# Logarithms of edge counts stored as they are computed, and copied into rows from DRAM to DRAM

## The chip, the cores and the metric

The kernel runs on one core of one Trainium2 chip. The metric is the device time of one execution in microseconds (us). A core has TensorE (PE; its weight loads are shown as PEld), VectorE (DVE), ScalarE (ACT), GpSimd (POOL) and SyncE (SP), and it is served by 16 DMA engines. SPq is SP's own queue of instructions, on which most of this kernel's transfers are issued. On-chip memories are SBUF and PSUM; DRAM is the large memory outside.

## The reference, cut to what matters

A graph of 3125 nodes and 100,000 edges passes through two blocks. Each block holds graph attention, a mixing layer and a feed-forward layer. Four graph attention layers run in all (one in block 0, three in block 1), and all of them use the same edges:

```python
loop = jnp.arange(N, dtype=edge_index.dtype)
src = jnp.concatenate([edge_index[0], loop])
dst = jnp.concatenate([edge_index[1], loop])
alpha = jax.nn.leaky_relu(a_src[src] + a_dst[dst], NEG_SLOPE)
m = jax.ops.segment_max(alpha, dst, num_segments=N)
alpha = jnp.exp(alpha - jax.lax.stop_gradient(m)[dst])
denom = jax.ops.segment_sum(alpha, dst, num_segments=N)
alpha = alpha / (denom[dst] + 1e-16)
out = jax.ops.segment_sum(h[src] * alpha[:, :, None], dst, num_segments=N)
...
x = x + _L0_gnn_ref(xn, ...) + _L0_mix_ref(xn[None], ...)[0]
x = x + _L0_ffn_ref(...)[0]
x = x + _L1_gnn_ref(...) + _L1_mix_ref(...)[0]
x = x + _L1_ffn_ref(...)[0]
```

## The kernel before, in words

The kernel turns the edge list into a dense matrix of 3125 x 3125 edge counts and works with it as a mask: for each pair of target d and source s it needs the negated logarithm of the count, and a very large number where there is no edge. That matrix ("lowered", 39 MB of fp32) is computed once and stored in DRAM. Each attention layer then reads it back in tiles of 125 targets (125 rows of 12,500 bytes, issued at L65 and L66, 50 pairs for each layer with two passes over the heads, 25 for the last layer).

The program is a row of stages. A stage ends when all engines have reached a barrier; SP reaches it after its own last wait. The stages that matter here, in order:

- "codes" and "keys" read the edges and make comparison codes.
- "counts" makes the matrix, one tile t of 125 targets at a time, 25 tiles. VectorE makes one-hot matrices (L303), TensorE multiplies them into counts in PSUM (L317, L320), ScalarE takes logarithm and mask of them (L336, L337) and VectorE subtracts the two (L296). The result is the SBUF tile nl[:, t % 2]: two buffers, each 125 partitions x 25 windows x 125. SP stores it. ScalarE may write tile t only when the store of tile t - 2 has landed in full.
- "general" does the same work for unusual edge lists; a flag tells that it is to be skipped, and with these inputs it is.
- "st0", "nm0", "g0p" and further stages of block 0 normalize, project and run the mixing layer. The first transfer that SP issues in them is the load of the projection's weights (g0p_w).
- "g0a" is the first attention layer (its `g.out` is "relu"). Its SP block begins with the loads of the first two tiles of "lowered".

How a tile is laid out decides the shape of its store. In SBUF, partition p = 25 e + s holds, for every window w and b, the element of target row 5 w + e (e from 0 to 4) and source column 125 s + b. In DRAM "lowered" is stored by rows of 3125. A partition's 3125 numbers thus belong to 25 different rows, and its store is 25 runs of 125 numbers, 500 bytes each. One tile is 3125 such runs, the whole matrix 78,125.

`tile_dma` (L63) splits each store into two transfers, of partitions 0 to 111 (L65) and of the last 13 (L66). `s.sem` makes a semaphore that the stage clears at its end. A transfer adds 16 to its semaphore when it has landed.

Within a stage each engine runs its instructions in the order of the code. SP's order is the order in which transfers enter its queue.

Of the kernel before, what the change touches and what calls it, by code (L numbers as in the profile page):

```python
# [13 lines left out]
N = 3125  # L14
R = 125
T = N // R
# [46 lines left out]
def tile_dma(eng, dst, src, sem):  # L63

    eng.dma_start(dst[0:CUT], src[0:CUT]).then_inc(sem, 16)  # L65
    eng.dma_start(dst[CUT:R], src[CUT:R]).then_inc(sem, 16)  # L66


def wait_apart(eng, tick, sem, value):

    eng.wait_ge(sem, value)
    eng.sem_inc(tick, 1)
# [20 lines left out]
W5 = 5  # L93
# [182 lines left out]
TINY = 2.0 ** -60  # L276


def stage_counts(nc, m, K, own, ownw, steps):

    with Stage(nc, "counts") as s:
        ohb, ohq = s.sb("ohb", [P, 2, 2, PAIRS, R, 2], BF16), s.sb("ohq", [P, 2, 2, PAIRS, QW, 2], BF16)
        nl, ln = s.sb("nl", [R, 2, T, R]), s.sb("ln", [R, 2, T, R])
        ps = s.ps("ps", 7)
        neg = s.sb("neg", [R, 2])
        hot, full, free, both_ready, nl_ready = s.sem("hot"), s.sem("full"), s.sem("free"), s.sem("both_ready"), s.sem("nl_ready")
        nl_out = [s.sem(f"nl_out{n}") for n in range(2)]
        block = s.block()

        @block.vector  # L290
        def _(dve):
            numbers = steps.unsqueeze(1).to_broadcast([P, PAIRS, R, 2])

            def lowered(t):
                dve.wait_ge(both_ready, t + 1)
                nc.vector.tensor_tensor(nl[:, t % 2], nl[:, t % 2], ln[:, t % 2], ALU.subtract).then_inc(nl_ready, 1)  # L296
            for t in range(T):
                if t > 1:
                    dve.wait_ge(full, (t - 1) * 7)
                for c in range(2):  # L300
                    for oh, c0 in ((ohq, 0), (ohb, 2)):
                        code = K[:, c0 + c, t, :].rearrange("p (x y) -> p x y", y=2).unsqueeze(2).to_broadcast([P, PAIRS, R, 2])
                        last = nc.vector.tensor_tensor(oh[:, t % 2, c], code, numbers, ALU.is_equal)  # L303
                last.then_inc(hot, 1)
                if t > 0:
                    lowered(t - 1)
            lowered(T - 1)

        @block.tensor
        def _(pe):  # L310
            for t in range(T):
                pe.wait_ge(hot, t + 1)
                for j, windows in JOBS:
                    w0, nw = windows[0], len(windows)
                    if t > 0:
                        pe.wait_ge(free, (t - 1) * 7 + j + 1)
                    nc.tensor.matmul(ps[0:R, j, 0:nw * R], own[:, t, :], ownw[:, w0:w0 + nw, :].rearrange("p w b -> p (w b)"), start=True, stop=False)  # L317
                    for x, w in enumerate(windows):
                        for c in range(2):
                            last = nc.tensor.matmul(ps[0:R, j, x * R:(x + 1) * R], ohq[:, t % 2, c, w // 2, :, w % 2], ohb[:, t % 2, c, w // 2, :, w % 2],  # L320
                                                    start=False, stop=(x == nw - 1 and c == 1))
                    last.then_inc(full, 1)

        @block.scalar
        def _(act):
            nc.scalar.activation(neg[:, 0:1], m.ones[0:R, 0:1], ACT.Copy, scale=NEG)
            nc.scalar.activation(neg[:, 1:2], m.ones[0:R, 0:1], ACT.Copy, scale=TINY)
            nc.scalar.drain()
            for t in range(T):
                if t > 1:  # L330
                    act.wait_ge(nl_out[t % 2], (t // 2) * 32)
                for j, windows in JOBS:
                    act.wait_ge(full, t * 7 + j + 1)
                    w0, nw = windows[0], len(windows)
                    counted = ps[0:R, j, 0:nw * R].rearrange("p (w b) -> p w b", b=R)
                    nc.scalar.activation(ln[:, t % 2, w0:w0 + nw, :], counted, ACT.Ln, bias=neg[:, 1:2])  # L336
                    nc.scalar.activation(nl[:, t % 2, w0:w0 + nw, :], counted, ACT.Relu, bias=neg[:, 0:1], scale=-NEG).then_inc(free, 1)  # L337
                nc.scalar.drain().then_inc(both_ready, 1)

        @block.sync  # L340
        def _(sp):
            for t in range(T):
                sp.wait_ge(nl_ready, t + 1)
                tile_dma(sp, m.NLQ[:, t], nl[:, t % 2], nl_out[t % 2])
            for n, x in enumerate(nl_out):
                sp.wait_ge(x, 32 * len(range(n, T, 2)))


def stage_counts_general(nc, m, wstart_rows):

    BLOCKS = (EDGES + CAP - 1) // CAP
    with Stage(nc, "general") as s:
        wstart = s.sb("wstart", [P, NW])
        e = s.sb("e", [P, 2, 2])
# [4 lines left out]
        tcol, own = s.sb("tcol", [R, T]), s.sb("own", [R, T])  # L359
        ps = s.ps("ps", 7)  # L360
        loaded, hot, full, added, zeroed = [s.sem(x) for x in ("loaded", "hot", "full", "added", "zeroed")]
        starts_in, counted, logged, finished, out = [s.sem(x) for x in ("starts_in", "counted", "logged", "finished", "out")]
        block = s.block()
        iota = m.iota[:, 0:R]
# [66 lines left out]
        def sp_part(sp):  # L431
            sp.dma_start(wstart[:], wstart_rows).then_inc(starts_in, 16)
            sp.sem_inc(out, 32)
            sp.sem_inc(added, 1)
            with sp.Fori(0, T) as t:
                with sp.Fori(0, BLOCKS) as r:
                    wait_apart(sp, s.tick, added, t * BLOCKS + r + 1)
                    wait_apart(sp, s.tick, zeroed, t + 1)
                    at = sp.snap(r * CAP)
                    sp.dma_start(e[:], m.QB[ds(at, CAP)].rearrange("(p c) k -> p c k", p=P)).then_inc(loaded, 16)  # L440
                wait_apart(sp, s.tick, finished, t + 1)
                tile_dma(sp, m.NLQ[:, ds(t, 1)].rearrange("p o w b -> p (o w) b"), nl[:], out)
            sp.wait_ge(out, 32 + 32 * T)

        @block.sync
        def _(sp):
            either(sp, sp_part)
# [384 lines left out]
def stage_gat_attend(nc, m, g, AL, HX, OUT, X=None, spare=None):  # L832
# [9 lines left out]
    with Stage(nc, g.name + "a") as s:  # L842
        als, nl = s.sb("als", [R, H, N]), s.sb("nl", [R, 2, N])
        as2 = s.sb("as2", [R, HG, N])[:] if spare is None else spare.rearrange("p (h n) -> p h n", h=HG)
        x = s.sb("x", [R, 3, N])
# [5 lines left out]
            low = s.sb("low", [R, 2, W])  # L851
        pst, pso = s.ps("pst", 6), s.ps("pso", 2)
        spread, als_ready = s.sem("spread"), s.sem("als_ready")
        nl_in = [s.sem(f"nl_in{p}") for p in range(2)]
        offset_ready, scaled, masked, exped, turned = [s.sem(n) for n in ("offset_ready", "scaled", "masked", "exped", "turned")]
        weighted, gathered, copied, inverted, rows_free = [s.sem(n) for n in ("weighted", "gathered", "copied", "inverted", "rows_free")]
# [60 lines left out]
        @block.sync  # L917
        def _(sp):
            def counts(gt, p):
                t = gt - gt // T * T if isinstance(gt, int) else gt  # L920
                tile_dma(sp, nl[:, p, :], m.NL[ds(t * R, R)], nl_in[p])
            counts(0, 0)
            counts(1, 1)
            for q in range(PASSES):
                with sp.Fori(0, T // 2 - 1) as i:
                    for p in range(2):
                        wait_apart(sp, s.tick, masked, (q * T + i * 2 + p + 1) * HG)
                        counts(i * 2 + p + 2, (q + p) % 2)
                for t in range(T - 3, T):
                    if q * T + t + 2 < PASSES * T and (t == T - 3 or q < PASSES - 1):  # L930
                        sp.wait_ge(masked, (q * T + t + 1) * HG)
                        counts(q * T + t + 2, (q + t) % 2)
# [222 lines left out]
def graph_attention(nc, m, g, AL, HX, OUT, X=None, spare=None):  # L1155

    stage_gat_attend(nc, m, g, AL, HX, OUT, X, spare)
# [1298 lines left out]
def build(nc, a, out):  # L2456
    m = Machine()
    m.src, m.dst = a["src"], a["dst"]

    def dram(name, shape, dt=F32):  # L2460
        return nc.dram_tensor(name, shape, dt).ap()
    m.QB = dram("edge_codes", [EDGES + CAP, 2])
    m.LO = dram("window_starts", [25, 25], I32)
    m.NL = dram("lowered", [N, N])
    m.NLQ = m.NL.rearrange("d s -> (d s)").rearrange("(t w p b) -> p t w b", t=T, w=T, p=R)
    m.XR, m.YR = dram("normal_rows", [N, D]), dram("expert_rows", [RESULTS, D])
    m.Y, m.XS = dram("attended", [N, 512]), dram("kept_rows", [R, T, D])
    with ExitStack() as ctx:
# [18 lines left out]
        with ExitStack() as cx:  # L2487
# [13 lines left out]
            with ExitStack() as c:  # L2501
                K, steps = sb("K", [P, 4, T, TE], BF16, c)[:], sb("steps", [P, R, 2], BF16, c)[:]
                own, ownw = sb("own", [P, T, R], BF16, c)[:], sb("ownw", [P, T, R], BF16, c)[:]
                stage_keys(nc, m, K, own, ownw, steps, X, x_rows, x_in)
                stage_counts(nc, m, K, own, ownw, steps)
            stage_counts_general(nc, m, a["c_wstart"])

            g0 = Gat("g0", 4, 64, "relu")
# [111 lines left out]
```

## Time and profile before

| | |
|---|---|
| time, median of 3 runs | 5261.91 us (5257.02 to 5267.69) |
| the profiled execution's own time | 5264.06 us |
| its span | 5262.4 us |
| PE / PEld busy | 4553.4 us (87%) / 4129.2 us (78%) |
| DVE busy | 3190.1 us (61%) |
| ACT busy | 2856.9 us (54%) |
| POOL busy | 1455.1 us (28%) |
| DMA queue of SP and ACT (q1) | 181,542 packets, 429.21 MB, 32.6% of 16 engines' time |
| packets under 512 bytes | 108,730 of 197,457 |

The profile was taken from one execution, and its times are inside that execution. A share of an engine's busy time is an average over the whole span. The stages differ, and the stage "counts" takes only about 6% of the span, from about 175 us (the first store) to about 467 us (the last store has landed). The DMA share of a stretch is the time in which the 16 DMA engines had a packet in work, divided by 16 times the stretch. Where packets of one engine overlap, it goes over 1.

### The profile page before, as it was taken

The page shows a single profiled execution, that of the slowest core. Times are in us where ns is not written, and L with a number is a line of the kernel's source. Part 1 is how long each engine was busy: PE and PEld are TensorE (multiplying, and loading weights), DVE is VectorE, ACT ScalarE, POOL GpSimd, SP SyncE. Part 2 cuts the span into 40 slices and gives each one's busy share as a digit, 9 for nine tenths or more (in the row PEclk, how much of TensorE's full clock was granted, in tenths as well). Part 3 has the DMA queues.
Part 4 walks back from the last instruction along what each step waited for, and adds up shares of the span by engine and source line. Part 5 has one row for each costly group of instructions (what it writes and reads, how often), then busy time and mean ns, then how long its engine had stood idle before and what let it go on. Part 6 is the DMA issues. An engine that isn't in the chain of part 4 may idle for free. (4 is left out here: it accounts for less than half of the span.)

```text
span 5262.4 us, 91302 instructions
## 1 busy us (share of the span) xinstructions
PE 4553.4 (87%) x34042; PEld 4129.2 (78%) x34042; DVE 3190.1 (61%) x2697; ACT 2856.9 (54%) x3889; POOL 1455.1 (28%) x1169
## 2 busy tenths in 40 slices
PE   1454669999999859987799999979999999799989
PEld 1443447999999858874489999977999999688755
DVE  4795230688888641116378888853888888255333
ACT  0563322577777523332157787752777877344332
POOL 3001000022222112220126666640566666100000
PEclk9776769899999879997899999989999999899989
DMA  2684000333333155542134434432444344354100
GB/s 49 95 134 77 5 18 0 84 96 96 96 96 96 37 175 173 174 140 50 43 86 104 104 96 104 104 78 64 109 104 104 94 104 104 101 139 115 33 17 20
DMA packets 197457, 462.87 MB, mean 88 GB/s; under 512 B 108730, under 2 KB 145579, under 8 KB 175126
## 3 DMA queue, kind: packets, MB, share of 16 engines
q1 hardware_dynamic: 181542, 429.21, 32.6%
q0 software_dynamic: 15296, 28.83, 2.3%
q8 instruction: 258, 4.23, 0.4%
q14 instruction: 73, 0.60, 0.0%
q10 hardware_dynamic: 288, 0.00, 0.0%
HBM read 388.28 MB, written 69.61 MB: 87 GB/s over the span
## 5 line engine op out<-in xcount | busy, mean ns | idle before, releaser
L1123 PE MATMUL g2a_pso<-HX,g2a_wt 125*125 125x129 f32 x5000 | 603.3, 274 | 7.2 <-DVEq L970 3.9
L1123 PE MATMUL g1a_pso<-HX,g1a_wt 125*125 125x129 f32 x5000 | 603.2, 275 | 4.6 <-ACT g1a_wt L1007 3.3
L1123 PE MATMUL g0a_pso<-HX,g0a_wt 125*125 125x65 f32 x5000 | 595.9, 274 | 5.9 <-ACT g0a_wt L1007 3.3
L1123 PEld LDWEIGHTS g0a_pso<-HX,g0a_wt 125*125 125x125 f32 x5000 | 586.0, 194 | 6.4 <-ACT g0a_wt L1007 3.4
L1123 PEld LDWEIGHTS g2a_pso<-HX,g2a_wt 125*125 125x125 f32 x5000 | 576.7, 189 | 7.6 <-DVEq L970 4.2
L1123 PEld LDWEIGHTS g1a_pso<-HX,g1a_wt 125*125 125x125 f32 x5000 | 576.9, 189 | 5.1 <-ACT g1a_wt L1007 3.5
L1007 ACT ACTIVATE g0a_wt<-g0a_pst 125x1000 f32<-125x1000 f32 (+1 forms) x300 | 312.0, 1040 | 199.8 <-PE g0a_pst L1110 199.8
L940 DVE SCALAR_TENSOR_TENSOR g0a_x<-g0a_als,g0a_cd,HX 125x3125 f32<-125x3125 f32 x100 | 347.5, 3475 | 111.2 <-PE g0a_pst L1110 102.0
L940 DVE SCALAR_TENSOR_TENSOR g2a_x<-g2a_als,g2a_cd,g2a_as 125x3125 f32<-125x3125 f32 x100 | 357.5, 3575 | 83.2 <-PE g2a_pst L1110 73.3
L940 DVE SCALAR_TENSOR_TENSOR g1a_x<-g1a_als,g1a_cd,g1a_as 125x3125 f32<-125x3125 f32 x100 | 358.2, 3582 | 80.6 <-PE g1a_pst L1110 70.4
L1007 ACT ACTIVATE g2a_wt<-g2a_pst 125x1000 f32<-125x1000 f32 (+1 forms) x300 | 312.2, 1041 | 169.6 <-PE g2a_pst L1110 169.6
L1007 ACT ACTIVATE g1a_wt<-g1a_pst 125x1000 f32<-125x1000 f32 (+1 forms) x300 | 312.2, 1041 | 169.5 <-PE g1a_pst L1110 169.5
L945 DVE CUSTOM_DVE_ANT_0 g1a_x<-g1a_x,g1a_nl 125x3125 f32<-125x3125 f32 x100 | 344.9, 3448 | 19.6 <-issue 13.9
L945 DVE CUSTOM_DVE_ANT_0 g2a_x<-g2a_x,g2a_nl 125x3125 f32<-125x3125 f32 x100 | 344.1, 3441 | 19.6 <-issue 13.9
L945 DVE CUSTOM_DVE_ANT_0 g0a_x<-g0a_x,g0a_nl 125x3125 f32<-125x3125 f32 x100 | 341.5, 3415 | 19.6 <-issue 13.9
L1110 PE MATMUL g0a_pst<-C,g0a_x 125*125 125x125 f32 x2500 | 346.0, 284 | 3.6 <-ACT g0a_x L999 3.6
L999 ACT ACTIVATE g2a_x<-g2a_x,g2a_top 125x1000 f32<-125x1000 f32 (+1 forms) x300 | 346.5, 1156 | 3.7 <-DVEq L947 3.7
L999 ACT ACTIVATE g0a_x<-g0a_x,g0a_top 125x1000 f32<-125x1000 f32 (+1 forms) x300 | 346.6, 1156 | 2.4 <-DVEq L947 2.4
L999 ACT ACTIVATE g1a_x<-g1a_x,g1a_top 125x1000 f32<-125x1000 f32 (+1 forms) x300 | 346.6, 1156 | 1.7 <-DVEq L947 1.7
L1110 PE MATMUL g1a_pst<-C,g1a_x 125*125 125x125 f32 x2500 | 323.0, 273 | 3.6 <-ACT g1a_x L999 3.6
L1110 PE MATMUL g2a_pst<-C,g2a_x 125*125 125x125 f32 x2500 | 322.5, 273 | 2.2 <-ACT g2a_x L999 2.2
L1110 PEld LDWEIGHTS g0a_pst<-C,g0a_x 125*125 125x125 f32 x2500 | 305.5, 194 | 3.8 <-ACT g0a_x L999 3.8
(454 smaller groups left out, 8201.5 us busy)
## 6 DMA issues: line engine op xcount, KB each, us to landing
g0a_nl<-lowered SPq DMA_DIRECT2D x50, 1367.2 KB
g1a_nl<-lowered SPq DMA_DIRECT2D x50, 1367.2 KB
g2a_nl<-lowered SPq DMA_DIRECT2D x50, 1367.2 KB
moe_wa<-in_L_ffn_W SPq DMA_DIRECT2D x56, 1024.0 KB, 5.2
lowered<-counts_nl SPq DMA_DIRECT2D x25, 1367.2 KB
g3a_nl<-lowered SPq DMA_DIRECT2D x25, 1367.2 KB
g0a_nl<-lowered SPq DMA_DIRECT2D x50, 158.7 KB
g1a_nl<-lowered SPq DMA_DIRECT2D x50, 158.7 KB
```

The source lines that it names most:

```text
L940: nc.vector.scalar_tensor_tensor(out=x[:, b, :], in0=als[:, h, :], scalar=cd[:, h:h + 1, ds(t, 1)].rearrange("p a b -> p (a b)"), in1=as2[ ...
L945: nc.vector.tensor_tensor_reduce(out=x[:, b, :], in0=x[:, b, :], in1=nl[:, (q + k // HG) % 2, :], scale=1.0, scalar=3e38, op0=ALU.add, op1 ...
L999: nc.scalar.activation(x[:, b, c0:c1], x[:, b, c0:c1], ACT.Exp, bias=top[:, b:b + 1], scale=-1.0).then_inc(exped, 1)
L1007: nc.scalar.activation(wt[:, side, 0:n * R].rearrange("p (b n) -> p b n", b=banks), pst[0:R, 3 * side:3 * side + banks, 0:per * R], ACT.Co ...
L1110: last = nc.tensor.transpose(pst[0:R, 3 * side + j // per, col:col + R], x[:, ring(q, k), (a0 + j) * R:(a0 + j + 1) * R], m.ident[0:R, 0:R])
L1123: last = nc.tensor.matmul(pso[0:R, unit(q, 0, k) % 2, 0:F + 1], wt[:, side, j * R:(j + 1) * R], HX[:, a, q * HG + k % HG, :], start=(a == ...
```

## The change

Four edits are made.

1. A second DRAM tensor, "computed", takes each tile as SBUF holds it: 125 partitions of 12,500 bytes each, one run for a partition. `m.NLQ` is now a view of it.
2. For each tile, five DRAM to DRAM copies (`copy_rows`, one for each e) move it from "computed" into the rows of "lowered". One copy is 25 windows x 25 parts s x 125 numbers: read as 625 runs of 500 bytes that lie 12,500 bytes apart, and written as 25 rows of 12,500 bytes. SP issues the copies of tile t - 1 behind the store of tile t, and first waits until the store of tile t - 1 has landed.
3. The copies count on a semaphore of their own (`by_row`), which outlives the stage. The stage's end no longer waits until the last data is in "lowered". The first attention layer waits for all 125 copies (16 x 5 x 25) before its first load.
4. The skipped stage "general" gets the same copies inside its branch.

```diff
+def copy_rows(sp, m, t, sem):
+    for e in range(W5):
+        sp.dma_start(m.NLR[t, e], m.NLD[t, e]).then_inc(sem, 16)
...
             for t in range(T):
                 sp.wait_ge(nl_ready, t + 1)
                 tile_dma(sp, m.NLQ[:, t], nl[:, t % 2], nl_out[t % 2])
-            for n, x in enumerate(nl_out):
-                sp.wait_ge(x, 32 * len(range(n, T, 2)))
+                if t > 0:
+                    sp.wait_ge(nl_out[(t - 1) % 2], ((t - 1) // 2 + 1) * 32)
+                    copy_rows(sp, m, t - 1, m.by_row)
+            sp.wait_ge(nl_out[(T - 1) % 2], ((T - 1) // 2 + 1) * 32)
+            copy_rows(sp, m, T - 1, m.by_row)
...
+        rows_again = s.sem("rows_again")
...
             sp.wait_ge(out, 32 + 32 * T)
+            sp.wait_ge(m.by_row, 16 * W5 * T)
+            for t in range(T):
+                copy_rows(sp, m, t, rows_again)
+            sp.wait_ge(rows_again, 16 * W5 * T)
...
+        first_layer = g.out == "relu"
+        if first_layer:
+            s.sems.append(m.by_row)
...
+            if first_layer:
+                sp.wait_ge(m.by_row, 16 * W5 * T)
             counts(0, 0)
             counts(1, 1)
...
     m.NL = dram("lowered", [N, N])
-    m.NLQ = m.NL.rearrange("d s -> (d s)").rearrange("(t w p b) -> p t w b", t=T, w=T, p=R)
+    computed = dram("computed", [N * N])
+    m.NLQ = computed.rearrange("(t p w b) -> p t w b", t=T, w=T, p=R)
+    m.NLD = computed.rearrange("(t e s w b) -> t e w s b", t=T, e=W5, s=T, w=T)
+    m.NLR = m.NL.rearrange("(t w e) (s b) -> t e w s b", t=T, e=W5, s=T)
+    m.by_row = nc.alloc_semaphore("by_row")
```

These are SP's instructions at the start of the stage "counts" before the change (a wait in brackets belongs to the instruction beside it; semaphores bear the name of their first user, so codes_counted stands for `nl_ready`, codes_summed and codes_prefix for the two of `nl_out`):

```order
L340 UNCONDITIONAL_BRANCH [waits barrier_Pool_Activation_PE_DVE_SP_release]
L65 DMA lowered<-counts_nl 112x25x125 [waits codes_counted]
L66 DMA lowered<-counts_nl 13x25x125
L65 DMA lowered<-counts_nl 112x25x125 [waits codes_counted]
L66 DMA lowered<-counts_nl 13x25x125
L65 DMA lowered<-counts_nl 112x25x125 [waits codes_counted]
```

And these are SP's instructions at the same place after it:

```order
L65 DMA computed<-counts_nl 112x3125 [waits codes_counted]
L66 DMA computed<-counts_nl 13x3125
L65 DMA computed<-counts_nl 112x3125 [waits codes_counted]
L66 DMA computed<-counts_nl 13x3125
L281 DMA lowered<-computed 25x25x125 [waits codes_summed]
L281 DMA lowered<-computed 25x25x125 x4
L65 DMA computed<-counts_nl 112x3125 [waits codes_counted]
L66 DMA computed<-counts_nl 13x3125
L281 DMA lowered<-computed 25x25x125 [waits codes_prefix]
L281 DMA lowered<-computed 25x25x125 x4
```

The stores lose their middle dimension of 25, and five copies of 25 x 25 x 125 stand between one tile's store and the next.

At the end of the stage, SP had this before:

```order
L65 DMA lowered<-counts_nl 112x25x125 [waits codes_counted]
L66 DMA lowered<-counts_nl 13x25x125
L57 UNCONDITIONAL_BRANCH [waits codes_prefix,codes_summed]
L445 UNCONDITIONAL_BRANCH [waits barrier_Pool_Activation_PE_DVE_SP_release]
L367 TENSOR_LOAD flag
```

and has this now:

```order
L65 DMA computed<-counts_nl 112x3125 [waits codes_counted]
L66 DMA computed<-counts_nl 13x3125
L281 DMA lowered<-computed 25x25x125 [waits codes_prefix]
L281 DMA lowered<-computed 25x25x125 x4
L281 DMA lowered<-computed 25x25x125 [waits codes_summed]
L281 DMA lowered<-computed 25x25x125 x4
L57 UNCONDITIONAL_BRANCH
L458 UNCONDITIONAL_BRANCH [waits barrier_Pool_Activation_PE_DVE_SP_release]
```

The ten copies of the last two tiles stand behind the last store, and the leave from the stage (L57) has no wait of its own any more.

## Rows read from the trace of the kernel before

**Rows 1.** Timeline of SP: start us, duration us; first two and last stores.

```profile
174.65 0.33 SPq L65 DMA_DIRECT2D lowered<-counts_nl  x1
175.02 4.36 SPq L66 DMA_DIRECT2D lowered<-counts_nl  x1
185.01 0.32 SPq L65 DMA_DIRECT2D lowered<-counts_nl  x1
...
455.53 0.32 SPq L65 DMA_DIRECT2D lowered<-counts_nl  x1
455.89 4.68 SPq L66 DMA_DIRECT2D lowered<-counts_nl  x1
```

**Rows 2.** Groups by line, 100 to 700 us: busy us, mean ns, idle before.

```profile
L303 DVE TENSOR_TENSOR counts_ohq<-K,steps 128x3250 bf16<-128x3250 bf16 x50 | 92.2, 1845 | 1.5 <-PEq L60 1.5
L303 DVE TENSOR_TENSOR counts_ohb<-K,steps 128x3250 bf16<-128x3250 bf16 x50 | 92.2, 1845 | 0.0
L296 DVE TENSOR_TENSOR counts_nl<-counts_nl,counts_ln 125x3125 f32<-125x3125 f32 x25 | 85.3, 3413 | 40.0 <-ACTq L338 39.9
```

**Rows 3.** Stretches: us, five engines busy (PE to POOL), clock, DMA share, GB/s.

```profile
175.00:300.00 125.00, 67.07 (x583) 56.59 (x584) 112.86 (x55) 78.01 (x148) 0.00 (x0) 0.73 0.88 136
300.00:462.00 162.00, 83.00 (x731) 70.25 (x729) 130.02 (x62) 96.63 (x182) 0.00 (x0) 0.72 0.86 134
```

**Rows 4.** Waits in 174 to 470 us: total, times, longest.

```profile
ACT counts_ln L336 <- DMA lowered<-counts_nl: 91.1, 21, 8.7
DVE counts_nl L296 <- ACTq L338: 39.9, 16, 9.8
```

**Rows 5.** Waits of SP's queue, 430 to 480 us.

```profile
SPq L57 <- DMA lowered<-counts_nl: 6.8, 1, 6.8
```

**Rows 6.** Timeline behind the stage "counts".

```profile
470.66 8.27 DVE L477 BATCH_NORM_STATS2 st_st<-X 125x6 f32<-125x256 f32 x25 [15.16 <-PEq L60]
493.73 0.83 SPq L722 DMA_DIRECT2D g0p_w<-in_L_gnn_W  x2
935.95 0.34 SPq L65 DMA_DIRECT2D g0a_nl<-lowered  x1
```

**Rows 7.** Stretches of the last store, the first g0a_nl loads, lina_rows loads (1 KB).

```profile
456.50:457.50 1.00, 0.00 (x0) 0.00 (x0) 0.00 (x0) 0.00 (x0) 0.00 (x0) 0.50 1.00 270
459.00:461.00 2.00, 0.00 (x0) 0.00 (x0) 0.00 (x0) 0.00 (x0) 0.00 (x0) 0.50 1.20 150
461.00:463.00 2.00, 0.00 (x0) 0.00 (x0) 0.00 (x0) 0.00 (x0) 0.00 (x0) 0.50 1.20 152
938.00:940.00 2.00, 1.67 (x15) 1.49 (x15) 0.00 (x0) 1.70 (x2) 0.00 (x0) 1.00 1.06 331
2435.50:2436.50 1.00, 0.00 (x0) 0.00 (x0) 0.90 (x2) 0.00 (x0) 0.00 (x0) 0.50 0.26 91
```

**Rows 8.** Stretches with transfers of 125 partitions alone (src/dst loads; edge codes store).

```profile
8.00:9.00 1.00, 0.00 (x0) 0.00 (x0) 0.00 (x0) 0.00 (x0) 0.00 (x0) 1.00 0.32 131
10.00:11.00 1.00, 0.00 (x0) 0.00 (x0) 0.00 (x0) 0.00 (x0) 0.00 (x0) 1.00 0.32 131
...
22.00:24.00 2.00, 0.00 (x0) 0.00 (x0) 1.55 (x3) 0.00 (x0) 0.00 (x0) 1.00 0.31 125
```

**Rows 9.** Timeline of SP: the loads of src and dst.

```profile
4.91 0.34 SPq L123 DMA_DIRECT2D codes_srci<-in_src  x1
5.30 0.30 SPq L124 DMA_DIRECT2D codes_dsti<-in_dst  x1
```

**Rows 10.** Stretches of the first store.

```profile
174.00:176.00 2.00, 0.00 (x0) 0.00 (x0) 2.00 (x2) 2.00 (x5) 0.00 (x0) 1.00 0.21 58
176.00:178.00 2.00, 0.00 (x0) 0.00 (x0) 2.00 (x2) 2.00 (x5) 0.00 (x0) 0.74 1.04 239
178.00:180.00 2.00, 0.00 (x0) 0.00 (x0) 2.00 (x3) 0.68 (x3) 0.00 (x0) 0.50 1.23 154
```

**Rows 11.** The page's DMA queues: packets, MB, share of 16 engines.

```profile
q1 hardware_dynamic: 181542, 429.21, 32.6%
```

## The prediction

> **What bounds the kernel now.** I read the page first. Over the whole span PE leads, but its share says nothing of the stage that is changed, so I went on to the waits, the groups, the stretches and SP's timeline of "counts" alone. The stores begin at 174.65 us and the last is issued at 455.53 us [rows 1]: 280.9 us for 24 tiles, 11.7 us for one. Two limits lie close together there. VectorE has 4 one-hot operations of 1.845 us and one subtraction of 3.413 us in each tile, 10.8 us [rows 2]. The DMA engines are at a share of 0.88 and 0.86, moving 136 and 134 GB/s [rows 3]. ScalarE waited 91.1 us for stores to land, and through it VectorE 39.9 us [rows 4]. So the stores of 500-byte runs do set the pace, but VectorE would take over as soon as they got faster: all that can be won inside the stage is 24 x (11.7 - 10.8) = 22 us. At the end SP waits 6.8 us for the last store [rows 5], and VectorE starts the next stage at 470.66 us [rows 6], 3.3 us after SP is free (455.89 + 4.68 + 6.8 = 467.4).
>
> **What a run costs.** The last store runs alone. Its steady part moves 150 and 152 GB/s over 16 engines [rows 7], so one engine needs 500 x 16 / 151,000 us = 53 ns for a run of 500 bytes. Its first microsecond shows 270 GB/s, or 30 ns.
>
> **The change part by part.**
>
> *The stores* become 125 runs of 12,500 bytes. With 112 partitions over 16 engines and 13 over 13, a busy engine gets 8 partitions, 100 KB. No row shows a store of that shape. The load of the same tile in g0a moves 331 GB/s, 20.7 GB/s for each engine [rows 7], which makes 4.8 us. The store of 125 partitions of edge codes moves 125 GB/s on few engines [rows 8], 25 GB/s each, which makes 4.0 us. I take W = 4.3 us, where the present stores take about 10 us. Taken alone this edit would give back at most the 22 us of the stage and some 5 us at its end.
>
> *The copies* are the heart of it. They bring back all 78,125 runs of 500 bytes, now from DRAM to DRAM, so the question is on how many engines they run. The transfers of 125 partitions in "codes" are the nearest rows: while the loads of src and dst, or the store of the edge codes, are alone, the share stands at 0.32 and 0.31 at 131 and 125 GB/s [rows 8]. That is 5 of 16 engines (0.3125), each fully busy. Stores of 112 partitions use all 16 (share 1.0 and above, rows 7). Five is the largest number up to 16 that divides 125, and 16 is the largest for 112. A copy has 25 windows as its outer dimension on both sides, and for 25 that number is 5 again. And it is the same five each time: src and dst were issued 0.4 us apart [rows 9], and two transfers on different engines would have shown twice the share. So I expect all 125 copies on the same five.
>
> The Trainium skill speaks against this change just there. "DMA: Bandwidth & Descriptors", section "Why a DMA increments its semaphore by 16 and not by 1", says that the number of engines is the largest up to 16 that divides the slowest dimension of both sides, and that the lowest-numbered ones are taken. By that rule, the trace's 0.31 and 0.32 agree with it for 125; that it also holds for copies from DRAM to DRAM with 25, no row of before shows.
>
> For one tile each of these five engines gets 5 x 625 / 5 = 625 runs. The cost of a run from DRAM to DRAM is in no row. Below it is bounded by the 30 ns of the fresh store; above by a read and a write in turn, 53 ns for the write and 47 ns for the read, for which the nearest row is the loads of 1 KB rows to 125 partitions (91 GB/s at share 0.26, so 91 x 0.3125 / 0.26 = 109 GB/s while busy, 22 GB/s for each engine, 47 ns for 1 KB; I take it whole). That makes 100 ns. I take 53 ns, the row with the same size and the same count. Reading and writing can overlap, and five engines press the memory less than sixteen, but each side is scattered, so I do not go below it. C = 625 x 0.053 = 33.1 us for a tile (18.8 us at 30 ns, 62.5 us at 100 ns).
>
> *What the copies hold up.* SP issues the store of tile t behind the copies of tile t - 2, in one queue, and on the five engines it runs behind them. ScalarE needs this store's buffer two tiles later (that is the wait of 91.1 us in rows 4, which now waits behind C). By then VectorE and ScalarE have long finished their 10.8 us. So the copies are not hidden beside the computation: the five engines work without a gap, and a tile takes C + W = 37.4 us in place of 11.7. The other eleven engines stand mostly idle.
>
> *The end of the stage.* SP no longer waits for the last copies, but it must have issued them. Beside the first store the row of L66 lasts 4.36 us [rows 1]: SP was let go at 179.4 us, when about 58 x 2 + 239 x 2 + 154 x 1.4 = 810 KB had moved [rows 10], which is 101 of the 175 runs of each engine. So SP is let go with some 75 runs of the transfer ahead outstanding. Before its last copy that leaves 75 + 125 = 200 runs for each engine, 10.6 us.
>
> *The added waits.* The wait for the store of tile t - 1 ahead of its copies is met by then, since that store lies in the queue ahead of the copies of tile t - 2. Behind it stand only the copies and the next store. The wait of the first attention layer stood at 935.95 us [rows 6] and moves back with everything; the copies have ended by then. Behind it stand the first two tile loads. It costs nothing. The load of g0p_w, 23 us after VectorE's start [rows 6], comes after the last copies too (10.6 us). The untaken branch costs nothing.
>
> **The sum.** The first copies are issued behind the second store (185.01 us, rows 1), which is through by about 190 us. From there: 25 x 33.1 = 828 us of copies and 23 stores x 4.3 = 99 us end at 1117 us; SP is free 10.6 us earlier, and VectorE begins the next stage 3.3 us after that, at 1110 us, against 470.66 us. The change costs 639 us. The profiled execution of before took 5264.06 us, which makes 5903 us; the median of the runs lies 2 us lower, so I predict 5901 us. At 30 ns: 190 + 469 + 99 - 6 + 3 = 755, 285 us more than now, 5547 us. At 100 ns: 190 + 1563 + 99 - 20 + 3 = 1835, 1364 us more than now, 6626 us.
>
> **The rivals.**
>
> *A. The copies use all 16 engines.* For it: nothing forbids it, and the 500-byte stores do. Against it: the 125-partition rows [rows 8]. Each engine has 195 runs, 10.4 us at 53 ns, and W is 4.8 us since all are at work, 15.2 us for a tile. End: 190 + 25 x 10.4 + 23 x 4.8 - 6 + 3 = 557 us, 87 us more than now, 5349 us.
>
> *B. The other side: the change pays.* The mechanism is the same as in A at a price of 30 ns: 195 x 0.030 + 4.8 = 10.7 us for a tile is below VectorE's 10.8 us, ScalarE's wait of 91.1 us goes, and the stage runs at VectorE's pace. That takes off about 20 us, 5242 us for the whole. It decides where the copies and the store of a tile fit into 11.7 us: below 35 ns for a run with 16 engines, below 12 ns with five. For it speaks only the 270 GB/s of one microsecond [rows 7]; the same row group shows 150 directly behind.
>
> *C. Stores pass the copies.* If a store did not stay behind the copies, the stage would run at VectorE's pace and the copies in its shadow, up to 190 + 828 + 99 = 1117 us. Then the first attention layer's wait is the one that counts: it stands at 936 us, and the whole costs 1117 - 936 = 181 us, 5443 us. Against it: all of these are transfers of SP's one queue q1 [rows 11], and SP itself stands for four microseconds when a transfer ahead is long [rows 1], so it could not even issue the next store.
>
> The Trainium skill has a rule on this, in "DMA: Bandwidth & Descriptors", section "Queues, rings and completion order": on each DMA engine the descriptors of a ring are taken in order, and SP owns one ring per engine. By that rule C falls away, and no row of before can show it, because there each transfer used all engines.
>
> **How the numbers follow.** The forecast of five engines that set the pace has a chance of 0.87, A 0.05, C 0.04 and B 0.04. About 0.2% (10 us) is what a measurement can tell from no change. A, C and the forecast are slower beyond it; B is faster, with 0.01 of it for a gain too small to see. So faster 0.03, same 0.01, slower 0.96. The range begins at the 30 ns end, 5547 us. On the other side I stop at 85 ns: C = 53.1 us, 190 + 1328 + 99 - 17 + 3 = 1603, 1132 us more, 6396 us. Left out are A, B and C (0.13) and prices over 85 ns (0.05).
>
> **What would show it.** In the profile after, "counts" should last from 175 to about 1106 us; the stores should be issued about 37 us apart; the DMA share there should be about 0.39 (5/16, and 11/16 of the 4.3 us in 37.4 us in which a store uses the others), and 0.31 while only copies run; copies and stores should each carry 1.56 MB in 37.4 us, 42 GB/s. ScalarE's wait for "computed" should grow from 91 us to some 600. SP's issues of L281 should last microseconds each. The wait of the attention layer should be zero, and everything from "st0" on should look as before, shifted. A DMA share near 1 in "counts" would be A; stores 11 us apart would be B or C, and C would show a wait of SP ahead of g0a_nl. If the share is right and the stores stand further than 37 us apart, only the price of a run was wrong.

## The result and the profile after

The changed kernel takes 5557.96 us in the median of four runs (5542.36 to 5568.87), against 5263.61 us before. The ratio is 1.0558, with a 95% interval of 1.053 to 1.0586. It is slower by 294 us, as forecast in direction and inside the range (5547 to 6396 us), but the forecast of 639 us more was over twice too large.

The profiled execution took 5558.1 us, with a span of 5556.5 us. The timeline of SP in the stage "counts" (start us, duration us) answers to [rows 1] and, with its first row of VectorE's next stage and the first load of "g0a", to [rows 6]:

```profile
185.12 0.32 SPq L65 DMA_DIRECT2D computed<-counts_nl  x1
185.48 0.39 SPq L66 DMA_DIRECT2D computed<-counts_nl  x1
185.92 17.77 SPq L281 DMA_DIRECT2D lowered<-computed  x5
203.74 3.90 SPq L65 DMA_DIRECT2D computed<-counts_nl  x1
...
716.99 3.46 SPq L65 DMA_DIRECT2D computed<-counts_nl  x1
720.50 0.39 SPq L66 DMA_DIRECT2D computed<-counts_nl  x1
720.94 37.46 SPq L281 DMA_DIRECT2D lowered<-computed  x10
...
765.88 8.27 DVE L490 BATCH_NORM_STATS2 st_st<-X 125x6 f32<-125x256 f32 x25 [71.89 <-PEq L60]
1230.72 0.34 SPq L65 DMA_DIRECT2D g0a_nl<-lowered  x1
```

Five copies keep SP for 18 to 20 us, and the stores stand 23.3 us apart, (716.99 - 203.74) / 22, where they stood 11.7 us apart [rows 1]. The next stage begins at 765.88 us, 295.2 us later than at 470.66 [rows 6]. That is the whole loss, as this table of first transfers shows:

| first transfer of | before | after | later by |
|---|---|---|---|
| projection (g0p_w) | 493.73 | 788.96 | 295.2 |
| feed-forward (mlp_wa) | 747.04 | 1041.19 | 294.2 |
| first attention (g0a_nl) | 935.95 | 1230.72 | 294.8 |
| second attention (g1a_nl) | 2667.73 | 2958.85 | 291.1 |
| output (out) | 5097.82 | 5391.87 | 294.1 |

The waits of the stage (total us, times, longest) answer to [rows 4]:

```profile
ACT counts_ln L341 <- DMA computed<-counts_nl: 332.8, 21, 16.5
DVE counts_nl L301 <- ACTq L343: 277.8, 22, 19.6
```

The same two waits have grown, by 242 and 238 us. The stretches (us, busy time of PE, PEld, DVE, ACT, POOL, clock, DMA share, GB/s) answer to [rows 3]. The second is behind the last store, where only copies run:

```profile
175.00:300.00 125.00, 44.56 (x399) 37.47 (x399) 76.06 (x37) 48.60 (x92) 0.00 (x0) 0.69 0.50 136
754.00:756.00 2.00, 0.00 (x0) 0.00 (x0) 0.00 (x0) 0.00 (x0) 0.00 (x0) 0.50 0.37 85
```

The DMA engines carry the same 136 GB/s as before, but now it is each byte twice, and at a share of 0.50 in place of 0.88. With copies alone the share is 0.37 at 85 GB/s. If five engines do it, each moves 17 GB/s, 29.4 ns for a run of 500 bytes (the stretches beside it lie between 80 and 85 GB/s, up to 31 ns); and 0.37 is 5/16 times 1.2, the same overlap of packets that gave 1.20 on sixteen engines [rows 7]. That it is five and not six without overlap, which would also be 0.37, is counted below.

The page's queue, answering to [rows 11]:

```profile
q1 hardware_dynamic: 185292, 468.28, 31.6%
```

39 MB more, yet hardly more packets: the 78,125 short runs have only moved from the stores to the copies.

### The profile page after: what moved, and what is told of

Its sections match the earlier page's. It is cut to its first block and busy times, and to the rows that moved or that the text cites. A ratio compares the mean times of both kernels' runs of the same rounds, so it can differ in the third digit from the quotient of the medians.

```text
span 5556.5 us, 91427 instructions
## 1 busy us (share of the span) xinstructions
PE 4556.1 (82%) x34042; PEld 4129.8 (74%) x34042; DVE 3191.8 (57%) x2697; ACT 2852.4 (51%) x3889; POOL 1455.0 (26%) x1169
## 5 line engine op out<-in xcount | busy, mean ns | idle before, releaser
L322 PE MATMUL counts_ps<-ownw,own 128*125 128x500 bf16 (+1 forms) x175 | 84.3, 482 | 353.5 <-ACT counts_nl L342 326.7
```

## The experiments

The later experiments ran on other chips than the first comparison; each is compared with runs of the kernel before on its own chip. Those lie at 5241 to 5244 us, and on the first chip at 5264 us; the last experiment shows where most of the difference lies. Where I compare stages, I give the start of the next stage (VectorE's L477 or what it became). It was 470.66 us in the first profile of before, and 452.18 us in the one profile of before that was taken on a later chip. The second is the one to compare the experiments with.

Three theories were to be told apart. "Memory": a short run costs 53 ns only because sixteen engines press on the memory at once, and five do not reach that limit. "Order": the copies' runs are cheap because they land side by side. "Source": a run from SBUF costs more than one from DRAM. "Memory" is only a name for what the engines share: no run here shows whether it is the DRAM itself or a path to it.

**The stores of before on five engines.**

```diff
-                tile_dma(sp, m.NLQ[:, t], nl[:, t % 2], nl_out[t % 2])
+                sp.dma_start(m.NLQ[:, t], nl[:, t % 2]).then_inc(nl_out[t % 2], 16)
```

(The two waits for `nl_out` count 16 in place of 32.)

> The kernel before, but each tile is stored by one transfer of 125 partitions in place of two of 112 and 13: the same scattered 500-byte runs from SBUF, now on five engines (share near 0.31). Theory 'memory': a run costs 30 ns as soon as only five engines are at it, 625 x 0.030 = 18.8 us per tile, 5440 us. Theory 'order' and theory 'source' (a run from SBUF costs 53 ns, one from DRAM 30): 33.1 us per tile, 5800 us.

5450.27 us, ratio 1.04 (1.037 to 1.043). A stretch of its stage, columns as above:

```profile
400.00:410.00 10.00, 3.73 (x30) 3.16 (x31) 3.77 (x3) 5.12 (x10) 0.00 (x0) 0.54 0.36 82
```

There is no copy and no second tensor here, just the scattered 500-byte runs of before, from SBUF. One transfer of 125 partitions in place of 112 and 13 brings the share to 0.36 and the rate to 82 GB/s, 30.5 ns for a run on five engines. These are the figures of the copies. ScalarE waits 272.8 us for the stores. "Order" and "source" had asked for 53 ns and 5800 us: both fall. It also confirms the divisor rule by an edit of its own.

The trace's packet records count the engines. The number of packets of 4 bytes on this queue in the stage fits one for each engine and transfer. Before there are 725, which is 25 times 16 + 13. Here there are 125, five for each of 25 transfers. The changed kernel has 1,350: the 725 of its stores and five for each of 125 copies.

**Copies with scattered writes.**

```diff
-    m.NLR = m.NL.rearrange("(t w e) (s b) -> t e w s b", t=T, e=W5, s=T)
+    m.NLR = m.NL.rearrange("(t w e) (s b) -> t e s w b", t=T, e=W5, s=T)
```

(`m.NLD` the same way.)

> The changed kernel with the two outer dimensions of each copy exchanged: still 25 x 25 runs on five engines, but an engine now reads 12,500 bytes side by side and writes 500-byte runs 62,500 bytes apart. Theories 'memory' and 'source': as the changed kernel, 18.8 us of copies per tile, 5558 us. Theory 'order': 53 ns for a run, 33.1 us of copies per tile, about 5910 us.

5551.73 us, ratio 1.0593 (1.0565 to 1.0622), beside 1.0558 for the changed kernel. The next stage begins at 757.38 us, 8 us earlier than with the changed kernel. It hardly matters on which side the runs are scattered, so "order" falls a second time.

**Copies cut into 16 and 9 windows.**

```diff
     for e in range(W5):
-        sp.dma_start(m.NLR[t, e], m.NLD[t, e]).then_inc(sem, 16)
+        for w0, w1 in ((0, 16), (16, T)):
+            sp.dma_start(m.NLR[t, e, w0:w1], m.NLD[t, e, w0:w1]).then_inc(sem, 16)
```

> Each copy of 25 windows is cut into one of 16 and one of 9. If a transfer runs on the largest number of engines up to 16 that divides its outer dimension, the halves run on 16 and on 9 engines, and the busiest engine has 250 runs of 500 bytes per tile in place of 625. Theory 'order' (a run costs 30 ns in the copies because runs land side by side): 250 x 0.030 = 7.5 us and 4.8 us for the store, 12.3 us per tile, end of the stage 17 us later than before the change: about 5280 us. Theory 'memory' (16 engines with short runs are held at 53 ns together, five are not): up to 13.3 + 4.8 = 18 us per tile, 5365 to 5425 us. If the copies were not bound to five engines, nothing changes: 5558 us.

5424.33 us, ratio 1.0352 (1.0329 to 1.0376); the next stage begins at 622.45 us. The stores stand 17.2 us apart, (581.11 - 185.14) / 23:

```profile
185.94 12.11 SPq L282 DMA_DIRECT2D lowered<-computed  x10
...
216.19 1.32 SPq L65 DMA_DIRECT2D computed<-counts_nl  x1
217.56 0.56 SPq L66 DMA_DIRECT2D computed<-counts_nl  x1
218.16 15.32 SPq L282 DMA_DIRECT2D lowered<-computed  x10
233.53 2.20 SPq L65 DMA_DIRECT2D computed<-counts_nl  x1
```

Twice as many transfers for the same data, and 143 us of the loss are gone in the trace (134 us in the medians). So the copies were bound by their outer dimension of 25; the stage has 3,850 packets of 4 bytes, 725 + 125 x (16 + 9). But the busiest engine's work fell from 625 to 250 runs, and the copies of a tile only from 18.4 to some 12.3 us. Now the engines are busy:

```profile
300.00:400.00 100.00, 38.68 (x342) 32.23 (x342) 58.66 (x29) 44.60 (x84) 0.00 (x0) 0.70 0.86 184
```

The price of a run has risen to some 50 ns. The total is what "memory" had expected at its upper end (5425 us), but that figure was worked out from the first chip's 5264 us. Against its own chip the kernel is 180 us slower, more than the 161 us of that end. So "memory" is right in kind, and its number is too low for copies.

**Cut into 20 and 5.** The same edit with `((0, 20), (20, T))`.

> Each copy of 25 windows is cut into one of 20 and one of 5. By the divisor rule they run on 10 and on 5 engines; the busiest engine has 375 runs of 500 bytes per tile. Theory 'memory' (all engines together get through some 300 runs per us, one engine alone through 33): 2500 runs at 300 per us are 8.3 us, 625 runs on five engines at 30 ns are 3.8 us, with the store 16.7 us per tile, about 125 us more than before the change. Theory 'busiest engine' (30 ns for each of its runs, whatever the others do): 11.3 + 4.6 = 15.9 us per tile, 105 us more. If neither held and only the number of copies counted, nothing would change: 310 us more.

5443.43 us, ratio 1.039 (1.0353 to 1.0427); the next stage begins at 646.01 us, 194 us later than 452.18, and the medians differ by 199 us. That is more than either theory gave (125 and 105 us), and less far from "memory". The stores stand 18.3 us apart, so the busiest engine's 375 runs take some 13.4 us, 36 ns each: ten engines do not run their parts at 30 ns each either. My number of 300 runs per us was too high for copies. That this is because a copy reads and writes DRAM, while the stores that gave the number only write it, is likely but was not tested.

**Cut into three parts.**

```diff
+        sp.dma_start(m.NLR[t, e, 0:16], m.NLD[t, e, 0:16]).then_inc(sem, 16)
+        for s0, s1 in ((0, 16), (16, T)):
+            to, frm = [x[t, e, 16:T, s0:s1].rearrange("w s b -> s w b") for x in (m.NLR, m.NLD)]
+            sp.dma_start(to, frm).then_inc(sem, 16)
```

> Each copy in three parts: 16 windows (16 engines), and of the other 9 windows the source parts s 0 to 15 (16 engines) and s 16 to 24 (9 engines). The busiest engine has 215 runs per tile in place of 250 (split in two) and 625; all engines together have 3125 as ever. Theory 'memory': with nearly all engines at work all the time, the total is held at some 240 to 300 runs per us whatever their spread, so the tile takes 15 to 17.5 us as with two parts, 150 to 180 us more than before. Theory 'busiest engine': the price per run is that of the engine, so the time falls with 215/250, by 1.8 us per tile and 45 us in all.

5386.09 us, ratio 1.0284 (1.0259 to 1.0308); stores 16.2 us apart, next stage at 594.01 us. It lies between the two: 1.0 us per tile against 0 and 1.8 us. The price of a run is neither fixed per engine nor a pure total. (This run was on another chip than the split in two, and the last experiment shows that chips differ.)

**Copies without rearrangement.** The masks then have their numbers in the wrong places.

```diff
-    m.NLD = computed.rearrange("(t e s w b) -> t e w s b", t=T, e=W5, s=T, w=T)
-    m.NLR = m.NL.rearrange("(t w e) (s b) -> t e w s b", t=T, e=W5, s=T)
+    m.NLD = computed.rearrange("(t e w f) -> t e w f", t=T, e=W5, w=T)
+    m.NLR = m.NL.rearrange("(t e w) f -> t e w f", t=T, e=W5)
```

> The changed kernel with copies of the same bytes on the same five engines, but without rearranging them: 25 runs of 12,500 bytes per copy on both sides (the masks of the attention layers are then in the wrong order, so their values differ). If bytes set the price at the 25 GB/s per engine of the 125-partition transfers: 312.5 KB per engine and tile, 12.5 us in place of 18.7, 5400 us. If only the number of runs did, the copies would cost under 1 us per tile: 5240 us. If DRAM to DRAM itself were held at the 84 GB/s seen in the copies: 5558 us.

5360.78 us, ratio 1.0229 (1.0201 to 1.0258). The theories of a price for each run alone (5240 us) and of a fixed rate from DRAM to DRAM (5558 us) fall. The first case (5400 us) is nearest: with copies alone the trace shows 94 to 156 GB/s, at its best nearly twice the 85 GB/s of the short runs.

```profile
561.00:563.00 2.00, 0.00 (x0) 0.00 (x0) 0.00 (x0) 0.00 (x0) 0.00 (x0) 0.50 0.36 156
565.00:567.00 2.00, 0.00 (x0) 0.00 (x0) 0.56 (x2) 0.60 (x1) 0.00 (x0) 0.50 0.36 156
```

On this chip the short runs with scattered writes took 5551.73 us, 308 us more than the kernel before. Of these, 191 us come from the shortness of the runs on five engines, and the other 117 us stay even with long ones.

This run also shows what holds a store up when SP is free. SP issues five copies in 3.65 us here. Yet the store that it issued at 503.71 us let ScalarE go on only 20.5 us later:

```profile
503.71 0.33 SPq L65 DMA_DIRECT2D computed<-counts_nl  x1
524.22 0.68 ACT L341 ACTIVATE counts_ln<-counts_ps,counts_neg 125x500 f32<-125x500 f32 x1 [8.38 <-DMA computed<-counts_nl]
```

In the version whose stage has only stores (below), one issued at 299.37 us has landed in full at 306.08 us.

**Copies on GpSimd's queue.** SP keeps its two last waits, and a block of GpSimd waits for each store and issues its five copies.

```diff
+        @block.gpsimd
+        def _(pool):
+            for t in range(T):
+                pool.wait_ge(nl_out[t % 2], (t // 2 + 1) * 32)
+                copy_rows(pool, m, t, m.by_row)
```

> The same 125 copies, issued by GpSimd on its own queue in place of SP's. Theory 'queue' (in the changed kernel a store waits because it stands behind copies in the same queue): the stores now pass, their distance falls from 23 us to 11 or 12 us; but the stage cannot end before GpSimd has issued its last copy, so the total hardly falls if five engines carry them (about 280 us more than before the change), and falls to some 90 us more if GpSimd's queue spreads them over 16 engines. Rival 'engines' (a store waits because the engines themselves are busy, whatever the queue): the stores stay 20 us or more apart.

5477.76 us, ratio 1.0455 (1.0418 to 1.0493). SP's timeline and GpSimd's later one:

```profile
294.99 0.32 SPq L65 DMA_DIRECT2D computed<-counts_nl  x1
295.35 0.56 SPq L66 DMA_DIRECT2D computed<-counts_nl  x1
305.35 0.32 SPq L65 DMA_DIRECT2D computed<-counts_nl  x1
305.72 0.66 SPq L66 DMA_DIRECT2D computed<-counts_nl  x1
319.24 0.32 SPq L65 DMA_DIRECT2D computed<-counts_nl  x1
...
607.96 9.57 POOL L281 DMA_DIRECT2D lowered<-computed  x8 [17.60 <-issue]
635.37 9.56 POOL L281 DMA_DIRECT2D lowered<-computed  x8 [17.84 <-issue]
```

The stores now pass: 10.4 to 14.5 us apart between 295 and 357 us, where they were 23.3. "Queue" holds: in the changed kernel a store stands behind copies because it is in their queue. And the stage still ends at 684 us (next stage), since GpSimd goes on issuing 8 copies every 27.4 us, 3.4 us for one.

The edit changed more than the queue, though. With copies alone the share is 0.88 here, where it was 0.37:

```profile
500.00:600.00 100.00, 0.00 (x0) 0.00 (x0) 0.00 (x0) 0.00 (x0) 36.21 (x31) 0.50 0.88 97
```

The packets are other ones too, of 4,500 and 4,000 bytes, and two thirds of the time ten or more of them are in work at once, so the copies no longer keep to the same five engines. The engines are busier than in the changed kernel (share 0.93 from 295 to 357 us, against 0.50) and the stores pass all the same, which speaks against "engines". But 97 GB/s is little more than the 85 GB/s of five engines: spreading them did not bring the 90 us of the expectation. What holds GpSimd's copies at this rate was not tested.

**All copies late.** The stage has only stores of long runs; pairs of (16, 9) windows are issued behind the loads of the first projection (35) and of the feed-forward layer (90).

> As e8, but all copies are issued late, 35 pairs behind the loads of the first projection and 90 behind those of the feed-forward layer: the stage has only its stores of 12,500-byte runs. My term 'the stores alone': stores 10.8 us apart, the next stage some 25 us earlier than before. The late copies need 91 us of 67 us and 234 us of 188 us, so about 24 + 46 us come back, and the whole is 45 us slower than before.

5350.73 us, ratio 1.0213 (1.0177 to 1.0249). The stores stand 10.4 us apart (299.37, 309.74, 320.11 us) and the next stage begins at 432.24 us, 20 us earlier than 452.18 (38 us earlier than in the first profile of before). The step "the stores alone" was right in kind: VectorE sets the pace then. The late copies cost more than expected: the kernel is 106 us slower than before, not 45 us. SP issues the 35 pairs in 94.2 us and the 90 pairs in 252.7 us, 2.7 and 2.8 us for one in place of 2.6, and the first attention layer starts at 1025.75 us.

**Two copies of five at once, the rest late, in two places and in three.**

```diff
+                    for e in range(2):
+                        copy_part(sp, m, t - 1, e)
...
+            if g.name == "g0":
+                copy_late(sp, m, 16)
...
+            if name == "mlp":
+                copy_late(sp, m, 100)
```

(`copy_part` issues one copy as the pair of 16 and 9 windows, `copy_late` the next n of those that are left: all of e = 2 to 4, and all five of the last tile.)

> Each copy is cut into 16 and 9 windows; two of the five copies of a tile are issued beside the next tile's store, and the others later, while the DMA engines idle: 16 pairs behind the loads of the first projection, 61 behind those of the feed-forward layer. From the split alone a pair costs 2.6 us, so a tile in the stage needs 4.8 + 5.2 = 10 us, just below VectorE's 10.8 us. If so, the stage goes at VectorE's pace: 15 to 27 us less than before, 0.3 to 0.5%. The late pairs need 42 us of the 67 us and 159 us of the 188 us of their stages and are hidden. If a pair costs over 3 us, both bounds are missed and the kernel is as slow as before or up to 30 us slower.

5234.62 us, ratio 0.9984 (0.997 to 0.9998). That is 10 us less than before, where 15 to 27 us were expected. The stage goes at VectorE's pace as forecast (next stage at 433.32 us), but the first projection takes longer, as the rows below show.

In the second version 8 of the 16 pairs move behind the loads of the mixing layer's product:

> As e8, but of the 16 pairs that stood behind the loads of the first projection 8 go behind the loads of the mixing layer's product. In e8 the projection's stage and what follows took 4.7 us more than before the change, with the copies at a DMA share of 0.87 in it. If the pairs cost time only where a stage has no room for them, these 4.7 us come back: 5230 us, 0.3% less than before. If they cost it by pressing on other traffic, it stays at e8's 5235 us.

5227.77 us against 5241.44 us, ratio 0.9977 (0.9964 to 0.999). SP's timeline in the version with two places shows how a tile fits:

```profile
299.21 0.34 SPq L65 DMA_DIRECT2D computed<-counts_nl  x1
299.60 0.40 SPq L66 DMA_DIRECT2D computed<-counts_nl  x1
300.04 5.92 SPq L281 DMA_DIRECT2D lowered<-computed  x4
309.58 0.34 SPq L65 DMA_DIRECT2D computed<-counts_nl  x1
```

10.4 us for a tile, and VectorE is busy 100.00 of 100 us from 200 to 300 us. These two versions are the only ones that beat the kernel before, by about 0.2%, and the interval of the first reaches to 0.9998. From the first projection's load to the next layer's the two-place version takes 76.1 us (456.40 to 532.51), the three-place one 71.0 us (456.31 to 527.28), and before 69.9 us: the copies cost time where they did not fit, as expected.

**The kernel before, once more.** Unchanged.

> The kernel before, unchanged, profiled on the chip of the later experiments, where its runs lie at 5225 to 5253 us against 5257 to 5268 us on the first chip. In e8's profile the first attention layer starts 30 us earlier than in the first profile of before, yet the total falls by only 10 us. If this is because the first chip's memory is slower with 500-byte runs, the stage's stores are here under 11.7 us apart and the stage ends earlier than 470 us. If it lies in the first attention layer, whose clock fell for a varying time between its passes (0.98, 0.95 and 0.91 granted over 200 us in three profiles), the stage is as on the first chip.

5241.47 us, ratio 1.0005 (0.999 to 1.0019). Its stage and its last store, columns as above:

```profile
175.00:300.00 125.00, 69.47 (x627) 58.98 (x627) 119.03 (x58) 82.44 (x157) 0.00 (x0) 0.75 0.81 145
...
442.00:444.00 2.00, 0.00 (x0) 0.00 (x0) 0.00 (x0) 0.00 (x0) 0.00 (x0) 0.50 1.22 188
444.00:446.00 2.00, 0.00 (x0) 0.00 (x0) 0.00 (x0) 0.00 (x0) 0.00 (x0) 0.50 1.21 184
```

The first case of the expectation holds. Here sixteen engines store short runs at 184 to 188 GB/s, 43 ns for a run, where the first chip had 150 to 152 GB/s [rows 7], 53 ns. SP had issued this last store by 443.04 us, so it is not the issuing that holds the rate. The stores stand 11.0 us apart, and the next stage begins at 452.18 us, 18.5 us earlier than on the first chip: that is most of the 22 us between the chips' times of before. Against this profile the three-place version (433.24 us) starts the next stage 18.9 us earlier, and 13.7 us of it are left in the medians.

## Why the prediction was wrong in size

**What bounds the kernel now.** Right. The gain that the stage can give was confirmed when the copies went away: stores 10.4 us apart. Only the pace of VectorE was 10.4 in place of 10.8 us: its instructions overlap a little, which a sum of their lengths leaves out (in the run without rearrangement three one-hot operations start at 503.60, 505.36 and 507.12 us and last 1.85 us each).

**Five engines.** Right, and shown, by the split into 16 and 9 (ratio 1.0352 from 1.0558), by the stores of before on five engines and by the count of 4-byte packets. The Trainium skill's rule in "DMA: Bandwidth & Descriptors", section "Why a DMA increments its semaphore by 16 and not by 1", had given this number; the trace's share of 0.37 at 85 GB/s for copies from DRAM to DRAM with 25 windows agrees with it.

**Stores stand behind the copies.** Right, and shown by GpSimd's queue, where they passed. That SP itself is held as well (23 of 23.3 us in the changed kernel) is not the whole cause: with long runs SP was free and a store still took 20.5 us. Rival C fell as expected.

**The cost of a run, the step that failed.** I took 53 ns, "the row with the same size and the same count", and C = 33.1 us. It is 29.4 ns (85 GB/s over five engines), so C = 18.4 us. The row had the right size of run but the wrong number of engines. 53 ns was not what an engine needs for a run, but the sixteenth part of the pace that all sixteen reach together (43 ns on another chip). The same stores on five engines cost 30.5 ns. I had written that "five engines press the memory less than sixteen" and then did not go below 53 because both sides are scattered; the experiment with exchanged dimensions shows that this hardly matters. The right row stood in the same group: 270 GB/s in the first microsecond of the store [rows 7], 30 ns. The prediction had it as its lower bound.

**The rest of the sum** holds with that one number. W comes out at 23.3 - 18.4 = 4.9 us (forecast 4.3); it is what is left of the tile, not measured by itself. (The upper end of the range, 6396 us, lacks the 2 us that the other sums take off; it should be 6394 us.) The copies end at 190 + 25 x 18.4 + 23 x 4.9 = 763 us, and the trace's DMA share falls between 764 and 766 us. SP is let go at 758.40 us, 200 runs x 29.4 ns = 5.9 us earlier than that. The wait of the attention layer costs nothing: its first load stands 294.8 us later, as everything does.

**One remainder.** The next stage begins 7.5 us after SP is let go, not 3.3 us [rows 5, 6]. In five of the experiments it is 7.4 to 9.0 us, in the three-place version, where SP is let go at 430.3 us, 2.9 us. The stage does not wait for copies in flight: without rearrangement it begins at 566.44 us with copies at 156 GB/s (row above), and in the three-place version they are in flight too:

```profile
429.00:431.00 2.00, 0.00 (x0) 0.00 (x0) 0.00 (x0) 0.00 (x0) 0.00 (x0) 0.50 0.87 182
```

What goes with the longer gap is a read of the queue "q14 instruction". In all six profiles that have the gap, a packet of 8,192 bytes of that queue starts 4.7 to 5.5 us after SP is let go, and the next stage 2.5 to 3.4 us behind it. In the three-place version, and where all copies are late (2.9 us as well), there is none in between. So the missing 4 us look like a wait for instructions. That was not tried by an edit, and why the read comes so late is open.

**The DMA share** was forecast at 0.39 and is 0.50. I had not counted that packets overlap by a factor of 1.2, as in [rows 7], nor that the tile is shorter.

## What to carry to other kernels

Read the price of a DMA run together with the number of engines that were at it: GB/s divided by the engines in use, and then ask whether the engines or the memory set it. A transfer whose outer dimension has only small divisors among the numbers up to 16 runs on few engines, 25 on five; the DMA share shows it (0.31 to 0.37 is five). Cutting the dimension into 16 and a rest is a cheap cure in part: here it took back 134 of the 294 us. Moving short runs from a store into a copy does not remove them; it pays only if they go where the engines and the queue are idle, and then no more than the next bound allows, here 0.2%.

## What the runs showed that was not expected

- Short runs on sixteen engines cost 53 ns on one chip and 43 ns on another, but on five engines 29.4 and 30.5 ns on the two chips where that was seen. A kernel bound by them differs between chips by 18.5 us in this stage.
- The first attention layer took 882 to 890 us in twelve profiles and 868 us in the three-place version, with the same instructions. The time goes with TensorE's granted clock. Over the layer's first 100 us the clock was 0.91 in the three-place version and 0.76 to 0.83 in the others (763 matmuls against 630 in the second profile of before). Behind a 3.3 us gap of TensorE between its passes it was 0.91 over 200 us in the three profiles of 890 us, and 0.95 or 0.98 in the rest. A single profile's total can therefore be off by 10 to 20 us, and the start of a stage is the better measure.

```profile
898.00:998.00 100.00, 93.44 (x763) 92.01 (x764) 81.88 (x39) 74.09 (x78) 13.19 (x10) 0.91 0.43 111
```

```profile
915.00:1015.00 100.00, 93.85 (x630) 92.35 (x630) 69.58 (x33) 62.70 (x65) 5.89 (x7) 0.76 0.38 95
```

The first of these two rows is from the three-place version, the second from the kernel before on the later chip; the last three numbers are clock, DMA share and GB/s.
